# Kept queries in a fused two-branch attention kernel: transposed in place of projected, with the loads of B's operands regrouped

## What is computed

```python
xn = _layernorm(x)
# branch A: 8 heads, latent of 32, head size 128 + 32
c_q, c_kv = xn @ W_DQ + b_DQ, xn @ W_DKV + b_DKV
q = concat(c_q @ W_UQ + b_UQ, c_q @ W_QR + b_QR)
k = concat(c_kv @ W_UK + b_UK, broadcast(xn @ W_KR + b_KR))
v = c_kv @ W_UV + b_UV
a = softmax(q @ k.T / sqrt(160)) @ v @ W_O + b_O
# branch B: 16 heads of 16, a mask from the queries
q, k, v = split(xn @ W_qkv)
sim = mean over heads of cosine(q, g);  scaled to 0..1 over all batches
pos = sim > 0.9       # tokens 0..4 of a batch belong to both sets
b = each token attends to the tokens of its own set, with its own softmax
out = x + a + b @ W_proj + b_proj
```

## Time and profile before

| | us |
|---|---|
| median of 3 runs (2919.12 to 2929.86) | 2926.73 |
| the profiled execution | 2920.25 |
| its span | 2918.4 |
| PE busy | 2788.8 (96%) |
| DVE busy | 2268.3 (78%) |
| ACT busy | 1649.1 (57%) |
| POOL busy | 1374.5 (47%) |
| mean granted clock of PE | 0.988 |

### The profile page before, as it was taken

The page is one execution under the profiler, slowest core; times in us unless marked ns, Lnnn a source line. Parts: engine busy times, 40 slices in busy tenths (PEclk is TensorE's granted clock), DMA queues, the critical chain, the costliest instruction groups (busy, mean ns, idle before and its releaser), DMA issues.

```text
span 2918.4 us, 45402 instructions
## 1 busy us (share of the span) xinstructions
PE 2788.8 (96%) x16881; PEld 1254.4 (43%) x16881; DVE 2268.3 (78%) x4167; ACT 1649.1 (57%) x1898; POOL 1374.5 (47%) x641
## 2 busy tenths in 40 slices
PE   6798899999999999999999999999999999999998
PEld 4653333443344443454334543444434544345433
DVE  5776787777877888778877788778887788777893
ACT  2344465555655556545665556555565456655675
POOL 6657422593216922197224942169221971249401
PEclk9999999999999999999999999999999999999999
DMA  5524225400344014521245013440145112550001
GB/s 174 181 52 91 69 75 115 92 18 32 97 102 84 18 46 117 118 36 39 61 113 109 21 32 97 102 84 20 43 122 114 36 39 61 112 109 21 18 15 38
DMA packets 128776, 213.17 MB, mean 73 GB/s; under 512 B 47648, under 2 KB 76320, under 8 KB 128380
## 3 DMA queue, kind: packets, MB, share of 16 engines
q1 hardware_dynamic: 124748, 202.93, 29.5%
q10 hardware_dynamic: 3808, 7.34, 0.7%
HBM read 138.04 MB, written 72.48 MB: 72 GB/s over the span
## 4 chain that ended last, share of the span: by engine, by line
PE 70%; DVE 12%; POOL 7%; DMA 5%; issue 3%; ACT 2%; SPq 1%; ACTq 0%; POOLq 0%; DVEq 0%
PE O L1253 20%; PE M L1140 12%; DVE mx L1488 9%; PE M L1134 8%; PE S L1238 7%; PE S L1241 6%; PE M L1168 4%; POOL PT L851 3%; POOL PTx L851 2%; PE M L1218 2%; PE M L1220 2%; PE M L1186 2%; DMA qk_d<-stg 2%; PE M L1180 2%; ACT PT L1004 1%
## 5 line engine op out<-in xcount | busy, mean ns | idle before, releaser
L1488 DVE TENSOR_REDUCE mx<-M 128x1 f32<-128x512 f32 x3072 | 1951.3, 682 | 378.6 <-PE M L1134 194.6
L1004 ACT ACTIVATE PT<-S 128x1024 f32<-128x1024 f32 x1280 | 1240.2, 1022 | 746.7 <-PE S L1241 472.6
L1140 PE MATMUL M<-KB,QB 50*128 50x512 f32 x2048 | 618.9, 477 | 29.8 <-DVE mx L1488 12.4
L1253 PE MATMUL O<-PT,VB 128*32 128x512 f32 x4096 | 547.5, 607 | 1.7 <-ACT PT L1004 1.7
L1140 PEld LDWEIGHTS M<-KB,QB 50*128 50x128 f32 x2048 | 253.2, 184 | 638.4 <-DVE mx L1488 323.8
L1134 PE MATMUL M<-KA,QA 98*128 98x512 f32 x1024 | 418.7, 458 | 17.6 <-DVE mx L1488 16.5
L1241 PE MATMUL S<-QB,KB 52*128 52x512 f32 x2048 | 376.7, 432 | 11.4 <-ACT PT L1004 7.9
L1004 ACT ACTIVATE PTx<-S 128x1024 f32<-128x1024 f32 x256 | 248.4, 1022 | 207.3 <-PE S L1238 152.8
L1238 PE MATMUL S<-QA,KA 114*128 114x512 f32 x1024 | 319.0, 413 | 13.8 <-ACT PTx L1004 6.3
L1134 PEld LDWEIGHTS M<-KA,QA 98*128 98x128 f32 x1024 | 173.6, 190 | 301.5 <-issue 241.8
L851 POOL TENSOR_TENSOR PT<-PT,PTx 128x2048 f32<-128x2048 f32 x64 | 292.3, 4573 | 21.3 <-POOL PT L851 9.9
(11 more groups left out here) (169 smaller groups left out, 2105.3 us busy)
## 6 DMA issues: line engine op xcount, KB each, us to landing
qk_d<-stg SPq DMA_DIRECT2D x32, 1024.0 KB
KA<-kt_d SPq DMA_DIRECT2D x48, 512.0 KB, 7.3
QB<-qk_d SPq DMA_DIRECT2D x192, 128.0 KB
KB<-qk_d SPq DMA_DIRECT2D x192, 128.0 KB
kt_d<-stg SPq DMA_DIRECT2D x16, 1024.0 KB
RB<-recb_d SPq DMA_DIRECT2D x63, 256.0 KB
PT<-in_x SPq DMA_DIRECT2D x8, 1024.0 KB, 7.5
RB<-rec_d SPq DMA_DIRECT2D x32, 256.0 KB
```

Of the source, the lines that this page charges most:

```text
L1004: nc.scalar.activation(probs(kind, of_a)[:, 2 * pair:2 * pair + 2, :], Sg[pair][:, :].rearrange("p (j s) -> p j s", j=2), ACT.Exp, scale=S ...
L1140: done = mm(m[:, :], QB[rows, 2 * q + a, at:at + P], KB[rows, 2 * q + a, keys], start=True, stop=True)
L1253: last = mm(O[32 * jj:32 * jj + 32, :], lhs, probs(kind, k)[:, jj, :], start=(c == 0), stop=(c == NC - 1), skip_group_check=True)
L1488: v.tensor_reduce(mx[:, g % 2, unit, kh:kh + 1], m[:, :], AX.X, ALU.max).then_inc(free, 1)
```

## The change

The queries of batches 1 to 7 that the first pass makes by tokens are kept: ACT copies each tile a second time (`q_half`, in `OA`'s place) and stores half a batch at a time from its own queue to `qt_d` (`keep_queries`). In group 1 of B, SP loads the next batch's queries (`load_qt`, into a part of `PTx`, which only A uses), and the fills qq0 and qq1 are four transposes a job. The keys (kk0, kk1) are projected as before, with 128 key channels each; batch 0 projects both. qk0 to qk3 thus become kk0, qq0, kk1, qq1 with one place to be stored for each side, and a quarter can be loaded only when both sides of its pair are stored.

`load_b` moves: quarters 0 and 1 in groups 6 and 7 of B, quarters 2 and 3 both in group 0 of A. In group 7 the store of the output and the load of the residual go ahead of the load, and the store of the last fill goes behind `recs`. In group 0 of B, `dens` of A's last group goes behind the shift and the loads. In the first A the whole order is rewritten: shifts earlier, denominators, `recs`, `scale` and the inversions on DVE later, Z filled within A. The values of A (`va`) are made by transposes, not by products with an identity. The layout of W_qkv on the host is the plain one.

```diff
@@ -37,7 +37,7 @@
 STEPS = STEPS_A + STEPS_B
-FILLS = ("cq", "kt0", "kt1", "qk0", "qk1", "qk2", "qk3")
+FILLS = ("cq", "kt0", "kt1", "kk0", "qq0", "kk1", "qq1")
 NF = len(FILLS)
@@ -128,7 +128,7 @@
         s[16][2] += [("va", 0)]
-        for at, name in ((20, "kt0"), (26, "kt1"), (34, "qk0"), (42, "qk1"), (50, "qk2"), (58, "qk3")):
+        for at, name in ((20, "kt0"), (26, "kt1"), (34, "kk0"), (42, "qq0"), (50, "kk1"), (58, "qq1")):
             s[at][2].append((name, 0))
...
@@ -271,7 +271,10 @@
     kt_d = dram("kt_d", [QA_, 2, P, S])
-    qk_d = dram("qk_d", [QB_, 2, P, S])
+    qq_d = dram("qq_d", [PACK, 2, P, S])
+    kk_d = dram("kk_d", [PACK, 2, P, S])
+    qt_d = dram("qt_d", [B, P, NC, D])
     sh_d = dram("sh_d", [2, 2, 16, P])
@@ -341,6 +344,10 @@
         return Sg[c // 2 % 2][:, c % 2 * HALF:c % 2 * HALF + D]
+    q_tok = PTx[:, 0].rearrange("p j c -> p (j c)").rearrange("p (c d) -> p c d", c=NC)
+    q_half = OA[:, :, :].rearrange("p f (c d) -> p f c d", c=4)
...
@@ -539,6 +549,15 @@
+        def load_qt(n, b):
+            if n == 1:
+                for f in range(2):
+                    wait_apart(sp, qt_out[f], (B - 1) * 16)
+            dn = dn_spot(b, QUADS - 1)
+            wait_apart(sp, m_full[dn.bank], dn.upto())
+            sp.dma_start(q_tok, qt_d[n]).then_inc(qt_in, 16)
         def store_fill(n, b, name):
...
@@ -562,10 +581,10 @@
         def load_b(n, q):
-            for side, dst, parts in ((0, QB, PART_Q), (1, KB, PART_K)):
+            for side, of, dst, parts in ((0, qq_d, QB, PART_Q), (1, kk_d, KB, PART_K)):
                 for e in range(2):
                     for i, part in enumerate(parts):
-                        src = qk_d[q, part, 64 * side:64 * side + 64].rearrange("(a e d) s -> e d a s", a=2, e=2)
+                        src = of[q // 2, part, 64 * (q % 2):64 * (q % 2) + 64].rearrange("(a e d) s -> e d a s", a=2, e=2)
                         rows = slice(64 * e + DB * i, 64 * e + DB * i + DB)
@@ -692,59 +711,74 @@
-        def a_steps(n, b, before):
+        def next_shift(n, b, g):
+            kind, nxt = ("a", g + 1) if g + 1 < GA else ("b", 0)
+            shift(n, kind, nxt, a_spot(n, b, ("fa", kind, nxt)))
+        def first_a():
+            leave_extremes()
+            next_shift(0, None, 0)
+            store_fill(0, None, "kk0")
+            leave_mask()
+            store_fill(0, None, "qq0")
+            next_shift(0, None, 1)
+            load_b(0, 0)
+            load_b(0, 1)
+            dens(0, "a", 0)
+            store_fill(0, None, "kk1")
+            next_shift(0, None, 2)
+            recs(0, "a", 0)
+            dens(0, "a", 1)
+            store_fill(0, None, "qq1")
+            load_b(0, 2)
+            recs(0, "a", 1)
+            dens(0, "a", 2)
+            wait_apart(sp, ones_in, 32)
+            next_shift(0, None, 3)
+            load_b(0, 3)
+            load_z(0)
+            recs(0, "a", 2)
+        def a_steps(n, b):
             for g in range(GA):
                 if g:
                     dens(n, "a", g - 1)
-                elif before:
+                else:
                     dens(b, "b", GB - 1)
-                kind, nxt = ("a", g + 1) if g + 1 < GA else ("b", 0)
-                if not before and g == 0:
-                    leave_extremes()
-                if not before and g == GA - 1:
-                    wait_apart(sp, ones_in, 32)
-                shift(n, kind, nxt, a_spot(n, b, ("fa", kind, nxt)))
-                if before:
-                    if g == 0:
-                        freed(b, 3)
-                        load_b(n, 3)
-                        load_z(n)
-                    if g == 2:
-                        store_out(b, 1, [a_spot(n, b, ("po", c)) for c in range(4, NC)])
-                elif g == 0:
-                    store_fill(0, None, "qk0")
-                    leave_mask()
-                    load_b(0, 0)
-                    store_fill(0, None, "qk1")
-                    load_b(0, 1)
+                next_shift(n, b, g)
+                if g == 0:
+                    freed(b, 3)
+                    load_b(n, 2)
+                    load_b(n, 3)
+                    load_z(n)
+                if g == 2:
+                    store_out(b, 1, [a_spot(n, b, ("po", c)) for c in range(4, NC)])
                 if g:
                     recs(n, "a", g - 1)
-                elif before:
+                else:
                     recs(b, "b", GB - 1)
-                if not before and g in (1, 2):
-                    store_fill(0, None, f"qk{g + 1}")
-                    load_b(0, g + 1)
...
                     dens(b, "b", g - 1)
-                else:
-                    dens(b, "a", GA - 1)
                 if g + 1 < GB:
...
                 if g == 0:
-                    if b == 0:
-                        load_z(b)
                     if not last:
...
                     load_residual(b, 0)
+                    dens(b, "a", GA - 1)
+                if g == 7:
+                    store_out(b, 0, [b_spot(b, last, ("po", c)) for c in range(4)])
+                    load_residual(b, 1)
                 if not last:
@@ -752,26 +786,27 @@
                         load_a(1)
-                    if g > 4:
-                        freed(b, g - 5)
-                        load_b(n, g - 5)
-                    if g >= 4:
-                        store_fill(n, b, f"qk{g - 4}")
-                if g == 7:
-                    store_out(b, 0, [b_spot(b, last, ("po", c)) for c in range(4)])
-                    load_residual(b, 1)
+                    if g == 1:
+                        load_qt(n, b)
+                    if g in (6, 7):
+                        freed(b, g - 6)
+                        load_b(n, g - 6)
+                    if 4 <= g < 7:
+                        store_fill(n, b, FILLS[g - 1])
                 if g:
                     recs(b, "b", g - 1)
                 else:
                     recs(b, "a", GA - 1)
+                if not last and g == 7:
+                    store_fill(n, b, "qq1")
                 if not last and g == 1:
...
-        a_steps(0, None, False)
+        first_a()
         for b in range(B - 1):
             b_steps(b, False)
-            a_steps(b + 1, b, True)
+            a_steps(b + 1, b)
         b_steps(B - 1, True)
@@ -887,15 +922,15 @@
                     scale(b, "b", GB - 1)
-                if i in (4, 6):
+                if not before and i in (0, 1, 3, 5):
+                    do_split(0, None, FILLS[3 + (0, 1, 3, 5).index(i)])
+                if not before and i == 6:
+                    clear_z(0)
+                if i in ((4, 6) if before else (5, 7)):
                     scale(n, "a", i // 2 - 2)
-                if not before and i in (0, 1, 3, 5):
-                    do_split(0, None, f"qk{(0, 1, 3, 5).index(i)}")
         def b_steps(b, last):
             n = b + 1
-            if b == 0:
-                clear_z(b)
             residual(b, 0)
@@ -910,7 +945,7 @@
                     if g >= 4:
-                        do_split(n, b, f"qk{g - 4}")
+                        do_split(n, b, FILLS[g - 1])
             residual(b, 1)
@@ -948,8 +983,17 @@
                 nc.scalar.activation(sq[:, f, c, :], Q2[i][:, 0:D], ACT.Square)
+                if b:
+                    if b > 1 and c == 0:
+                        act.wait_ge(qt_out[f], (b - 1) * 16)
+                    nc.scalar.activation(q_half[:, f, c, :], Q2[i][:, 0:D], ACT.Copy).then_inc(qt_kept[f], 1)
                 at = b * (NC * HB) + HB * (4 * f + c)
                 nc.scalar.activation(dots[:, at:at + HB], Q2[i][:, D:D + HB], ACT.Copy).then_inc(q_used[i], 1)
+        def keep_queries(b, f):
+            act.wait_ge(qt_kept[f], b * 4)
+            act.dma_start(qt_d[b, :, 4 * f:4 * f + 4, :], q_half[:, f]).then_inc(qt_out[f], 16)
@@ -971,12 +1015,16 @@
                     keep(b + 1, 0)
+                if b:
+                    keep_queries(b, 0)
                 if b + 2 < B:
...
                     keep(b + 1, 1)
+                if b:
+                    keep_queries(b, 1)
                 fills(sum(PREP_OF[4 * b:4 * b + 4], []), prep_spot, 0)
@@ -1012,6 +1060,9 @@
             if kind == "a":
+                if n == 0:
+                    act.wait_ge(qt_out[q], (B - 1) * 16)
                 nc.scalar.activation(OA[:, q, cols], O[:, :], ACT.Copy).then_inc(o_free, 1)
@@ -1162,10 +1213,19 @@
                 done = mm(m[:, :], lhs, latT[0:LAT + 1, hf * HALF:(hf + 1) * HALF], start=True, stop=True)
-            elif kind[:2] == "qk":
-                q, hf = int(kind[2]), j[1]
+            elif kind[:2] == "qq" and b is not None:
+                t, hf = int(kind[2]), j[1]
+                if t == 0 and hf == 0:
+                    pe.wait_ge(qt_in, n * 16)
+                for c in range(4):
+                    done = nc.tensor.transpose(m[:, c * P:(c + 1) * P], q_tok[:, 4 * hf + c, P * t:P * t + P],
```

(22 more changed lines are left out.)

## The result

The changed kernel takes 2968.24 us (median of 4 runs, 2959.47 to 2972.07), the kernel before 2928.30 in the same sessions (4 runs, 2919.12 to 2930.77): a ratio of 1.0136, with a 95% interval of 1.0113 to 1.0160. It is slower by 40 us. The forecast was 2992 with 2935 to 3025, so the sign and the range were right and the size was too large. The profiled execution took 2959.47 us with a span of 2957.7.

A forecast was written before the change was run, and what follows sets the result against it. PE bounds B; A hangs on PE and POOL's sums. Chain delay 12.8 less surviving gain 3.2 plus clock 1.4 makes 11.0 us a batch, 77 in seven; 2920.25 + 77 - 9 + 4 = 2992 us, range 2935 to 3025.

The forecast's parts named there:

- The place and the mechanism: Head of A: SP waits for two loads and fills Z before the reciprocals; their late broadcast stalls POOL about 10 us.
- What PE gains: Queries transposed instead of projected, and VA in single-pass matmuls, save PE 5.5 us a batch, 39 us in the kernel.
- The split into swallowed and surviving gain: Per batch, 3.2 us saved between A's step 12 and B's step 57 survives; the last two jobs' 2.3 is lost.
- The chain's size: From B's late groups through SP to A's broadcast of reciprocals: 14.7 us later by the sum, set at 12.8.
- two of the terms: In SP's chain, the store of the last queries (7.5 us) and denominators to first load (6.48); 2 us taken off.
- the 1.5 that I set for the residual ahead of the load: B's group 7: the residual issued before the load was to add 1.5 us to the load's 14.62.
- The terms for the two loads: A's group 0: first load 14.62 us, the second not running beside it and adding 12.1 us.
- the faster rival: A's group 0: second load lands within the first's time, POOL doesn't wait, 2876 us; chance 0.11.
- The clock: In each A, PE idling in the new wait loses clock: 1.4 us a batch, half of batch 0's 2.7.
- the late gain: PE's saving in a batch's last two query jobs, after B's step 57, swallowed by SP's chain: 2.3 us a batch.
- Batch 0 and the first pass: Batch 0's A: PE's shift wait and lost clock go, 9 us off; first pass: query copies add 4 us.
- The successor that I named: Batch 0, B's step 6: store of A's last denominators late behind loads of xn and residual; nothing, bounds -5 and +5.

The follow-up runs named there:

- the two orders of the reciprocals: Changed kernel with the reciprocals of B's last group sent after both loads but before SP's wait and Z's fill: 2929.87 us; or between the loads: 2904.83 us.
- the second profile: The changed kernel run once more, unaltered, to learn its own spread: 2973.93 us, ratio 1.0157 against the kernel before.
- the last kernel: Changed kernel with reciprocals between A's two loads, quarter 1's load behind the last queries' store, batch 0's small transfers ahead of loads: 2861.52 us, ratio 0.9782.

## Why the prediction was right, and where its sizes were off

**The place and the mechanism: right.** What was to be seen is there: two loads in a row in A's group 0, the fill of Z behind both, POOL idle 10.67 us ("about 10") in front of the rescaling, A of batch 3 11.6 us longer ("some 10"), B 5.5 shorter ("3 to 5"), the clock below 1 in A. The kernel with the load move alone shows it to be the cause, and the two orders of the reciprocals show both halves of it, the wait and the queue.

**What PE gains: right.** Counted from the first product with the values to that of the next step, a step with one of the two middle query jobs fell from 4.25 to 3.30 us, one with a late job from 4.71 to 3.42, VA's step from 4.52 to 3.33: 2 x 0.95 + 2 x 1.29 + 1.19 = 5.67 us a batch; the forecast had 5.5, and 0.9 for the jobs where VectorE nearly fills the step. The rows after, for the two kinds of term:

```profile
1504.90 0.66 PE L1222 MATMUL M<-ident,PTx 128*128 128x128 f32 x4
1505.49 0.74 PE L1301 MATMUL S<-QB,KB 52*128 52x512 f32 x4
1508.79 0.73 PE L1301 MATMUL S<-QB,KB 52*128 52x512 f32 x4
...
1566.82 0.60 PE L1222 MATMUL M<-ident,PTx 128*128 128x128 f32 x4
1567.35 0.73 PE L1301 MATMUL S<-QB,KB 52*128 52x512 f32 x4
```

Four transposes take 0.53 to 0.59 us to the next score matmul (0.58 was taken from the earlier trace rows).

**The split into swallowed and surviving gain: right.** The kernel with qq1 projected again tells it: 18 us of PE's work more, and the same time.

**The chain's size: too large.** Its terms, one by one, in batch 3 (forecast, then measured from the rows above):

```
output's store and its landing       3.03    3.06
residual's issue                     0.48    0.52
load, to where the recs' store lands 16.12  14.55
broadcast's issue                    0.6     0.71
store of the last queries            7.5     6.00
denominators to the load             6.48    4.18
two loads                           26.72   26.50
Z, then to the recs' store           4.80    4.40
recs' store to broadcast             2.13    2.13
broadcast's landing                  3.71    4.07
sum                                 71.5    66.1
```

The same stretch took 56.8 before (1216.46 to 1273.30), so the delay is 9.3 us, not the 12.8 of the sum (14.7 less 2 is 12.7; the forecast wrote 12.8). What was mis-sized first is the step "two of the terms hold waits behind other transfers that are partly gone; I take 2 off". Together the two fell by 3.8: 1.5 of the 7.5 and 2.3 of the 6.48. And the 1.5 that I set for the residual ahead of the load was no cost either. The terms for the two loads, on which the argument hung, came out within 0.3 us. The second load took the first's rate: 26.50 - 14.62 = 11.9 us (12.1 worked out from the earlier trace rows). Windows of 10 us while both run, after (same columns as the earlier trace rows):

```profile
1248.00:1258.00 10.00, 8.71 (x42) 4.30 (x40) 6.89 (x12) 3.88 (x4) 9.45 (x3) 1.00 0.98 148
1258.00:1268.00 10.00, 9.08 (x54) 4.30 (x53) 6.79 (x13) 5.64 (x6) 9.73 (x3) 1.00 1.04 142
```

The share is 0.98 and 1.04 with two loads issued, as it was 1.02 with one; so the faster rival (they overlap) is out. The Trainium skill ("SBUF — State Buffer", on the DMA port swizzle) has 16 partitions at 104 GB/s and two transfers at once serialising. That they serialise agrees. The rate does not: 148 and 142 GB/s in these windows, and 1.64 MB in 11.9 us for the second load, so that the estimate of 15.8 us from the page's figure was 3.9 too high.

**The clock: at most half of what I gave it.** It falls in the new wait, as forecast (two windows after, over the wait and right behind it):

```profile
1280.00:1292.00 12.00, 6.98 (x24) 3.97 (x22) 3.44 (x7) 0.00 (x0) 6.95 (x3) 0.77 0.09 26
1292.00:1300.00 8.00, 6.81 (x26) 4.36 (x27) 3.13 (x6) 3.88 (x4) 7.45 (x3) 0.71 0.00 0
```

But there POOL paces the steps: ACT waits 2.87 us for POOL's sum at 1296.93, at half clock, and 2.90 at full clock elsewhere, as before. The two steps behind the wait took 10.5 us before and 0.2 to 1.2 more after, 0.7 in the mean over seven batches (1.1 in the second profile); the forecast had 1.4. Even that doesn't reach A's end: from the start of POOL's rescaling to the end of A it is 81.1 us before, 80.5 after and 80.8 in the second profile (means of seven), for PE, having run ahead, is ready when ACT is let go. The Trainium skill ("TensorE: Matmul & The Clock Gate", on oscillation) has the clock fall at every such wait of a loop. It does, in each of the seven As (granted 0.92 to 0.97 over an A); that each would pay in full, 2.7 us, is not what they show, since another engine was slower than PE at half clock just then.

**A batch, put together.** The seven As grew by 12.1 each. Of this 2.6 is the late gain, which brings A's start forward but not the chain, so that delay and clock together are 9.5 (forecast 14.2). POOL's rescaling comes 12.7 us later after A's start than before (52.6 against 39.9, means of seven), and what follows is 0.6 shorter: all of A's growth is the late broadcast. The Bs' remaining gain is 6.1 - 2.6 = 3.5 (forecast 3.2). Net 6.0, where the forecast had 11.0; seven times the difference is 35 us, and more than all of the miss in the spans (72 forecast, 39.3 measured).

**Batch 0 and the first pass.** PE's wait of 6.25 us for the shifts of group 2 is gone: that step took 12.78 us and takes 5.05, and with the step behind it 16.64 became 8.12. I had 9 us for it with its clock, and 8.5 it was. But I had 0 for what comes late next, and A of batch 0 gained only 5.8: its last step, from score to score, takes 9.91 us where it took 6.21. What comes late there is not what I named but the same thing once more: the shift to B's first group. It stands behind A's last denominators and a store of reciprocals, and that store was issued right behind the load of quarter 2 and took 8.2 us (297.47 to 305.65). In the timeline after, it is PE's wait for B's first scores. The successor that I named, A's last denominators behind the load of xn, is there as well, as a wait of VectorE:

```profile
314.59 1.22 PE L1301 MATMUL S<-QB,KB 52*128 52x512 f32 x4 [6.85 <-DMA QB<-sh_d]
...
346.61 1.29 DVE L1593 COPY latT<-M 128x512 f32<-128x512 f32 x2 [7.12 <-DMA den_d<-latT]
```

The step of B with the second of them took 13.89 us before, when it waited for Z, and takes 11.13 now, so it was no loss against the before. B of batch 0 gained 6.7, about 1 more than the query jobs and VA give (5.67); the same B takes 221.0 to 227.5 us in the five profiles whose batch 0 has the changed kernel's order and jobs, so this 1 tells nothing. In the last kernel, which sends both small transfers ahead, A's last step takes 2.88 us and the step of B 6.20, which bears out the place of both. The first pass was set at 4 us; the profiles give 3 to 8.

## What to carry to other kernels

In a queue whose order is written by hand, a bulk load that is put in front of a small transfer can cost in two ways: the issuing engine waits for its landing (38 us here, in seven batches), and the small transfer queues behind its bytes (25 us for the second load). Price it at the engine that stands at the far end (here PE, by way of POOL and ACT), and put the loads behind. Work saved on the busiest engine counts only between the points where the chain runs on it: of 5.67 us a batch, the 2.6 that lay behind the last point before a timed chain was worth nothing. With the queue mended A is bound by PE again, so that it should count in full; no run shows that by itself. When a term of a sum is an interval from the old trace, ask how much of it was work and how much was a wait behind something that the change takes away.

## What the runs showed of the hardware that I had not expected

A small transfer waited for nearly the whole of the load that had been issued before it on the same queue: the reciprocals' store, issued 6.94 us after the load's first transfer (1229.17 against 1222.23), was seen as landed only 14.55 us after it, as late as the load itself would have been (14.62 in the earlier trace rows). And half clock cost by who sets the pace. Over the kernel it rose from about 70 us to about 130 (worked out from the mean granted clocks, 0.988 and 0.978), while behind the wait in A, where ACT waits for POOL, the rest of A took no longer than before (80.5 against 81.1 us). In batch 0's B, where PE was busy throughout, four steps took 17.93 us at a granted clock of 0.54 and 12.79 at 1.00.
